# A graph attention kernel: one of four masks per row tile made by ScalarE, another moved from step 4 to step 6

## The chip, the core and the metric

The kernel runs on one core of a Trainium2 chip. The core has five engines that run side by side, each through its own queue of instructions in program order: TensorE (PE in the rows; PEld is its weight load), VectorE (DVE), ScalarE (ACT), GpSimd (POOL) and SyncE (SP), which here only issues DMAs. They meet through semaphores: an instruction adds to one when it is done, and `wait_ge` holds an engine's whole queue until a count is reached. The metric is the time of the kernel on the device in microseconds (us), lower is better.

## The reference

Two graph attention layers over N = 6144 nodes with 128 features, each followed by a sum with its input and a layer norm:

```python
# layer 0
scores = jnp.where(adj > 0, einsum('md,de,ne->mn', x, weight, inp), NEG_PAD)
x = _layernorm(x + jax.nn.softmax(scores / 0.07, axis=1) @ inp)
# layer 1
Wh = x @ W
e = leaky_relu((Wh @ a1)[:, None] + (Wh @ a2)[None, :], 0.2)
att = jax.nn.softmax(jnp.where(adj > 0, e, -9e15), axis=1)
x = _layernorm(x + jax.nn.elu(att @ Wh))
```

`adj` is a 6144 x 6144 matrix of int32 zeros and ones.

## The kernel before

The first part does layer 0, the second, over six groups of 1024 rows, layer 1. The change is in the first part.

**Tiles and steps.** Layer 0 runs over 48 row tiles of 128 rows (`t`), and each tile in 12 steps (`c`) of 512 columns. A tile's work is spread over three passes of the loop, so that in pass `t` the engines work on several tiles: TensorE makes the scores of tile `t` (L563 to L565, three products, since x and z are held as a high and a low float16 part), ScalarE takes the exponential of tile `t-1` (L717), and TensorE transposes the probabilities of a chunk three steps later (L552), ScalarE copies the transposed chunk from PSUM as a high part `pT_hi` (L706), VectorE makes the low part `pT_lo` (L866), and TensorE multiplies both with the values `vals` two steps after the transpose (L528, L530). Blocks 0 to 2 of each tile are turned by DMA instead (`moved_hi`, L711 on ScalarE, `moved_lo`, L417 on GpSimd), so steps 3 to 5 have no transposes on TensorE.

**Masks.** `adj` comes in four quarters of 1536 columns into `adj_sb`. VectorE turns each into `neg_mask` (L830): 0 where there is an edge, -2^60 where there is none. L857, one instruction for two chunks of 512 (a pair, at each odd step), adds mask and scores, writes `rows` and gives a maximum. In pass `t` the masks of quarters 2 and 3 of tile `t` are made at steps 0 and 2, those of quarters 0 and 1 of tile `t+1` at steps 4 and 10. GpSimd makes `edges` from each mask (L394, one byte for each element), which SyncE stores to DRAM for layer 1. `mask_set` counts masks in their order, and SyncE loads the next tile's quarter when the mask of this one is made.

**The end of a tile.** At the last step VectorE takes the row maximum and makes `exp_bias` (L916, L920), for which the exponential of step 0 waits. TensorE's transposes need `pT_lo` of two transposing steps before, since `ps` has two banks for them:

```python
pe.wait_ge(exp_set, C * (t - off) + bc + 1)
after(pe, pT_lo_set, n + 1 - NPT)
```

**The sum of products.** All 12 blocks of a tile are summed in one bank, block 3 first and block 2 last. When they are through, ScalarE copies the bank to `att` at step 8 (`ATT_STEP`, L699). The first block of the next tile is due in the same step 8, and starts the bank afresh:

```python
if bc == MOVED:
    after(pe, att_out, t_of)
```

From `att` VectorE makes the sum with x (L895, L899, step 9), and the statistics (L903 to L908, step 10); GpSimd takes the power -0.5 (L434), and VectorE normalizes at step 0 of the next pass (L911). These run from pass 2 on.

The order of all engines is the order of the code; nothing reorders it.

Of the kernel before, what the change touches and what calls it, by code (L numbers as in the profile page):

```python
# [6 lines left out]
P = 128  # L7
CHUNK = 512
QUARTERS = 4
# [15 lines left out]
EPS = 1e-5  # L25
SPLIT_SCALE = 64.0
MASK_BIG = 2.0 ** 60
PROB_SHIFT = 14 * math.log(2.0)

ALU = mybir.AluOpType  # L30
# [6 lines left out]
def build(nc, x, adj, inp, w0, w1, a1, a2, edge_rows, out):  # L37
# [17 lines left out]
    with ExitStack() as ctx:  # L55
# [19 lines left out]
        s_prod = sb("s_prod", [P, 2, P], F32)  # L75
        a21 = sb("a21", [P, 2], F32)
        consts = sb("consts", [P, GT], F32)
        s_top = sb("s_top", [P, 2], F32)

        def sb0(name, shape, dt):  # L80
# [1 line left out]

        zT = sb0("zT", [P, 2, N], F16)
        adj_sb = sb0("adj_sb", [P, QUARTERS, QW], I32)
        neg_mask = sb0("neg_mask", [P, QUARTERS, QW], BF16)
        neg_mask_row = neg_mask[:].rearrange("p q w -> p (q w)")
        edges = sb0("edges", [P, QUARTERS, QW // 2], U16)
        edge_bytes = edges[:].bitcast(U8)
        vals = sb0("vals", [P, NB, 2 * P], F16)
# [106 lines left out]
        xq_in = sem("xq_in")  # L196
        xr_in = [sem(f"xr_in{i}") for i in range(2)]
        const_set = sem("const_set")
        ident_set = sem("ident_set")
        wT_turned = sem("wT_turned")  # L200
        wT_copied = sem("wT_copied")
# [171 lines left out]
        def _(pool):  # L373
            nc.gpsimd.memset(ident[:], 0.0).then_inc(const_set, 1)
            nc.gpsimd.memset(consts[:], -0.5).then_inc(const_set, 1)
            nc.gpsimd.memset(averager[:], 1.0 / P).then_inc(avg_set, 1)
            nc.gpsimd.memset(w1_c[:, P:P + 1], 1.0 / P).then_inc(avg_set, 1)
            pool.wait_ge(const_set, 2)
# [11 lines left out]
            def make_edges(t, q):  # L390

                after(pool, edges_out[q], 16 * t)
                pool.wait_ge(mask_set, QUARTERS * t + q + 1)
                nc.gpsimd.tensor_scalar(edge_bytes[:, q, :], neg_mask[:, q, :], 1.0 / MASK_BIG, 1.0, ALU.mult,  # L394
                                        ALU.add).then_inc(edges_set, 1)

            for q in range(QUARTERS // 2):
                make_edges(0, q)
# [21 lines left out]
            def tile_rstd(t, par, known):  # L420
                ahead = t < NB - 1
                if t < NB:
                    make_edges(t, 2)
                if t >= 3:
                    score_cols(t - 3)
                if t < NB:
                    make_edges(t, 3)
                if 1 <= t <= NB:
                    moved_low(t - 1)
                if ahead:  # L430
                    make_edges(t + 1, 0)
                if ends_tile(known):
                    pool.wait_ge(ve_set, t - 1)
                    nc.gpsimd.tensor_tensor(small[:, 4:5], small[:, 3:4], consts[:, 0:1], ALU.pow).then_inc(rstd_set, 1)  # L434
                if ahead:
                    make_edges(t + 1, 1)

            tiles(pool, tile_rstd)

# [216 lines left out]

        @block.scalar
        def _(act):
            act.wait_ge(wT_turned, 1)
            nc.scalar.copy(w0T, ps[:, MISC, 0:P])  # L660
            nc.scalar.copy(w1T, ps[:, MISC, P:2 * P]).then_inc(wT_copied, 1)
# [26 lines left out]
            def tile_steps(t, par, known):  # L688
                for c in range(C):
# [10 lines left out]
                    if turn_at(known, c):  # L700
                        off, bc = turn_of(t, c)
                        n = turn_number(t - off, bc)
                        act.wait_ge(turned, n + 1)
                        if n >= PT_SLOTS:
                            act.wait_ge(pv_done, attend_number((n - PT_SLOTS) // TURNS, (n - PT_SLOTS) % TURNS + MOVED) + 1)
                        nc.scalar.copy(pT_hi[:, n % PT_SLOTS, :], ps[:, PT0 + n % NPT, :]).then_inc(pT_hi_set, 1)  # L706
                    if c == MOVED and 1 <= t <= NB:
                        act.wait_ge(exp_set, C * (t - 1) + MOVED)
                        if t >= 2:
                            act.wait_ge(movedT_in[t % 2], movedT_loads(t - 2))  # L710
                        nc.scalar.copy(moved_hi[:], rows[:, (1 - par) * N:(1 - par) * N + MOVED * CHUNK]).then_inc(moved_hi_set, 1)  # L711
# [88 lines left out]
        def _(dve):  # L800
# [23 lines left out]
            def make_mask(t, q, known):  # L824

                dve.wait_ge(adj_in[q], 16 * (t + 1))

                after(dve, masked, PAIRS * (t - 1) + pairs_of(q) if known != 0 else 0)
                after(dve, edges_set, QUARTERS * (t - 1) + q + 1 if known != 0 else 0)
                nc.vector.tensor_scalar(neg_mask[:, q, :], adj_sb[:, q, :], 0.0, -MASK_BIG, ALU.is_le,  # L830
                                        ALU.mult).then_inc(mask_set, 1)

            xT_low(0, 0)
# [4 lines left out]
            def tile_steps(t, par, known):  # L838
                for c in range(C):
# [5 lines left out]
                    if scores_of(known) and c % 2 == 1:  # L845
# [8 lines left out]
                        if k == 0:  # L854
                            after(dve, max_set, t)
                        dve.wait_ge(scored, C * t + c + 1)
                        nc.vector.tensor_tensor_reduce(row_pair(par, k), scores_pair(k),  # L857
                                                       neg_mask_row[:, 2 * k * CHUNK:2 * (k + 1) * CHUNK], 1.0, -3.0e38,
                                                       ALU.add, ALU.max, part_max[:, k:k + 1]).then_inc(masked, 1)
                    if turn_at(known, c):  # L860

                        off, bc = turn_of(t, c)
# [11 lines left out]
                    else:  # L874
                        if c in (0, 2) and scores_of(known):
                            make_mask(t, 2 + c // 2, known)
                        if c in (4, 10) and (known is None or known < NB - 1):
                            make_mask(t + 1, c // 10, None)
                    if c == x_step(known) and (known is None or known < NB - 1):
                        xT_low(t + 1, 1 - par)  # L880
                    if ends_tile(known):
# [180 lines left out]
```

## Time and profile before

| what | value |
|---|---|
| time, median of 3 runs | 1532.46 us (1532.19 to 1532.89) |
| the profiled execution | 1532.11 us, span 1530.3 us |
| TensorE busy | 1442.6 us, 94% of the span, granted clock 0.992 |
| VectorE busy | 1308.3 us, 85% |
| ScalarE busy | 1065.1 us, 70% |
| GpSimd busy | 1009.0 us, 66% |
| chain that ended last | TensorE 70%, VectorE 16%, issue 6%, GpSimd 3% |

The span runs from the first to the last instruction; the time has some 2 us around it. An engine can be busy for most of the span without being the bound, and TensorE's matmuls are pipelined, so its share alone doesn't say how near it is to its limit. The page's 40 slices show two parts: up to slice 26 (about 1000 us) the DMA engines are busy for 0.8 to 0.9 of the time at some 235 GB/s, with the loads of `adj`; after that for 0.2 to 0.5. A busy time of one instruction on ScalarE or VectorE is up to 0.1 us longer than the distance from its start to the next one's, since they overlap a little.

### The profile page before, as it was taken

What the parts mean: (1) busy time and instruction counts of PE and PEld (TensorE: products, weight loads), DVE (VectorE), ACT (ScalarE), POOL (GpSimd) and SP (SyncE); (2) the same over time, 40 slices, a digit from 0 to 9 for tenths busy, and PEclk for the clock granted to TensorE, in tenths of its full rate; (3) what the DMA queues carried; (4) which work ended last, traced back from release to release, by engine and by line L of the source; (5) the groups of instructions that cost most, each with busy time, mean ns of one, the idle gap of its engine ahead of it and who ended that gap; (6) DMA issues with size and microseconds to landing.
All of it is one profiled execution on the core that took longest, in us unless ns stands there. A gap on an engine that the chain in (4) does not pass through costs nothing.

```text
span 1530.3 us, 28253 instructions
## 1 busy us (share of the span) xinstructions
PE 1442.6 (94%) x9853; PEld 1030.4 (67%) x9853; DVE 1308.3 (85%) x2303; ACT 1065.1 (70%) x2327; POOL 1009.0 (66%) x628
## 2 busy tenths in 40 slices
PE   7799999999999999999999999987999999999996
PEld 3477777777777777777777777765566666666664
DVE  6988889988888998888998888976869797979794
ACT  4577887777787777787777787787745454646363
POOL 6545555555555555555555555535999999999995
PEclk9999999999999999999999999998999999999998
DMA  7888888888889988898888898826323534353420
GB/s 243 255 218 249 232 233 243 240 215 242 238 238 222 250 222 236 243 236 231 243 232 225 245 230 234 242 67 128 86 63 70 111 76 108 82 109 80 103 55 14
DMA packets 378749, 278.81 MB, mean 182 GB/s; under 512 B 307696, under 2 KB 354032, under 8 KB 378608
## 3 DMA queue, kind: packets, MB, share of 16 engines
q1 hardware_dynamic: 378608, 277.01, 69.1%
q8 instruction: 79, 1.29, 0.3%
q14 instruction: 62, 0.51, 0.1%
HBM read 160.56 MB, written 40.89 MB: 132 GB/s over the span
## 4 chain that ended last, share of the span: by engine, by line
PE 70%; DVE 16%; issue 6%; POOL 3%; ACT 1%; DVEq 0%; ACTq 0%; POOLq 0%
PE ps L612 11%; PE ps L528 11%; PE ps L605 10%; PE ps L552 9%; PE ps L565 6%; PE ps L564 6%; PE ps L563 6%; DVE pT_lo L866 6%; PE ps L530 5%; PE ps L589 5%; DVE rows L857 4%; DVE neg_mask L830 3%; POOL p_lo L449 2%; DVE xr L895 1%; PE ps L623 1%
## 5 line engine op out<-in xcount | busy, mean ns | idle before, releaser
L717 ACT ACTIVATE rows<-rows,exp_bias 128x512 f32<-128x512 f32 x576 | 415.2, 721 | 81.5 <-DVE exp_bias L920 81.5
L857 DVE CUSTOM_DVE_ANT_0 rows<-ps,neg_mask 128x1024 f32<-128x1024 f32 x288 | 350.7, 1218 | 99.7 <-PE ps L565 99.1
L449 POOL TENSOR_TENSOR p_lo<-p,p_hi 128x1024 fp32r<-128x1024 f32 x180 | 424.3, 2394 | 13.2 <-PE ps L589 7.7
L947 DVE SCALAR_TENSOR_TENSOR p<-ps,e_col,edgesT 128x1024 f32<-128x1024 f32 x288 | 349.0, 1276 | 62.2 <-PE ps L582 37.5
L394 POOL TENSOR_SCALAR edges<-neg_mask 128x1536 uint8<-128x1536 bf16 x192 | 284.4, 1481 | 145.2 <-DVE neg_mask L830 137.3
L706 ACT CAST pT_hi<-ps 128x512 f16<-128x512 f32 x432 | 252.0, 583 | 129.6 <-PE ps L552 121.6
L528 PE MATMUL ps<-vals,pT_hi 128*128 128x256 f16 x1728 | 331.4, 273 | 1.2 <-ACT att L699 0.8
L530 PE MATMUL ps<-vals,pT_lo 128*128 128x128 f16 x1728 | 308.3, 219 | 0.0
L746 ACT CAST p_hi<-p 128x1024 fp32r<-128x1024 f32 x180 | 185.0, 1047 | 176.5 <-DVE p L947 174.4
L552 PE MATMUL ps<-ident,rows 128*128 128x128 f32 x1728 | 263.0, 275 | 39.7 <-DVE pT_lo L866 39.0
L866 DVE TENSOR_TENSOR pT_lo<-ps,pT_hi 128x512 f16<-128x512 f32 x432 | 287.1, 682 | 8.7 <-ACT pT_hi L706 8.7
L434 POOL TENSOR_TENSOR small<-small,consts 128x1 f32<-128x1 f32 x48 | 26.6, 555 | 320.4 <-DVE small L908 320.4
L563 PE MATMUL ps<-zT,xT_hi 128*128 128x512 f16 x576 | 218.9, 380 | 6.9 <-DVE vals L816 4.2
L552 PEld LDWEIGHTS ps<-ident,rows 128*128 128x128 f32 x1728 | 184.4, 141 | 54.0 <-issue 45.8
L564 PE MATMUL ps<-zT,xT_hi 128*128 128x512 f16 x576 | 218.8, 380 | 0.0
L565 PE MATMUL ps<-zT,xT_lo 128*128 128x512 f16 x576 | 218.8, 380 | 0.0
L528 PEld LDWEIGHTS ps<-vals,pT_hi 128*128 128x128 f16 x1728 | 169.1, 98 | 65.9 <-DVE pT_lo L866 1.9
L612 PE MATMUL ps<-p,vals 128*128 128x512 f32 x432 | 204.5, 596 | 0.0
L530 PEld LDWEIGHTS ps<-vals,pT_lo 128*128 128x128 f16 x1728 | 169.1, 98 | 49.4
L830 DVE TENSOR_SCALAR neg_mask<-adj_sb 128x1536 bf16<-128x1536 int32 x192 | 201.3, 1048 | 0.5 <-POOL edges L394 0.3
L417 POOL TENSOR_TENSOR moved_lo<-rows,moved_hi 128x1536 f16<-128x1536 f32 x48 | 176.4, 3675 | 6.5 <-ACT moved_hi L711 2.7
L605 PE MATMUL ps<-p_hi,vals_hi 128*128 128x512 f32 x360 | 157.9, 519 | 6.7 <-POOL vals_lo L445 4.1
(108 smaller groups left out, 1785.6 us busy)
## 6 DMA issues: line engine op xcount, KB each, us to landing
adj_sb<-adj SPq DMA_DIRECT2D x192, 768.0 KB, 4.9
edge_rows<-edges SPq DMA_DIRECT2D x192, 192.0 KB, 4.4
rows<-inp SPq DMA_DIRECT2D x4, 768.0 KB, 9.0
xq<-x SPq DMA_DIRECT2D x48, 64.0 KB, 2.7
xr<-x SPq DMA_DIRECT2D x48, 64.0 KB, 1.9
out<-y_w SPq DMA_DIRECT2D x5, 512.0 KB, 3.7
movedT<-moved_hi SPq DMA_TRANSPOSE x48, 5.5
movedT<-moved_lo SPq DMA_TRANSPOSE x48, 3.8
```

The lines of the kernel that those rows point to most:

```text
L449: nc.gpsimd.tensor_tensor(p1_lo[:, m % LO_SLOTS, :], p1[:, (NB * g + n) % P_SLOTS, :], p1_hi[:, m % HI_SLOTS, :].bitcast(F32), ALU.subtrac ...
L528: nc.tensor.matmul(acc, p_hi, vals[:, jb, :], start=(bc == MOVED and b == 0), stop=False, skip_group_check=True)
L530: mm = nc.tensor.matmul(acc[:, P:2 * P], p_lo, vals[:, jb, 0:P], start=False, stop=(bc == MOVED - 1 and b == BPC - 1), skip_group_check=True)
L552: mm = nc.tensor.transpose(ps[:, PT0 + n % NPT, b * P:(b + 1) * P], rows[:, pb * N + bc * CHUNK + b * P:pb * N + bc * CHUNK + (b + 1) * P] ...
L563: nc.tensor.matmul(scores_bank(c), xT_hi[:, par, :], zT[:, 0, cols], start=True, stop=False)
L564: nc.tensor.matmul(scores_bank(c), xT_hi[:, par, :], zT[:, 1, cols], start=False, stop=False)
L605: mm = nc.tensor.matmul(acc_half(g % 2, i), v[:, k, :], p1_hi[:, m % HI_SLOTS, i * CHUNK:(i + 1) * CHUNK], start=(n == 0 and v is vals1_hi ...
L612: mm = nc.tensor.matmul(acc_half(g % 2, i), vals1[:, n, :], p1[:, (NB * g + n) % P_SLOTS, i * CHUNK:(i + 1) * CHUNK], start=(n == 0), stop ...
L717: nc.scalar.activation(row_chunk(1 - par, c), row_chunk(1 - par, c), ACT.Exp, bias=exp_bias[:, 1 - par:2 - par], scale=EXP_SCALE, accum_ou ...
L857: nc.vector.tensor_tensor_reduce(row_pair(par, k), scores_pair(k), neg_mask_row[:, 2 * k * CHUNK:2 * (k + 1) * CHUNK], 1.0, -3.0e38, ALU.a ...
L866: nc.vector.tensor_tensor(pT_lo[:, s, :], ps[:, PT0 + n % NPT, :], pT_hi[:, s, :], ALU.subtract).then_inc(pT_lo_set, 1)
L947: nc.vector.scalar_tensor_tensor(out=p1[:, (NB * g + n) % P_SLOTS, :], in0=ps[:, R_ROW:R_ROW + 2, :].rearrange("p b w -> p (b w)"), scalar ...
```

## The change

Four things change. The mask is positive: `off_mask` is +2^60 where there is no edge, and L857 (L870 after) subtracts it. GpSimd makes `edges` by one comparison (at most 0) in place of a product and a sum. From pass 1 to pass 46 the mask of quarter 1 of tile `t+1` is made by ScalarE, as Relu(2^60 - 2^60 x adj), at step 7 between `pT_hi` and the exponential, with the constant in a column `big_col`; VectorE no longer makes it at step 10. VectorE's mask of quarter 0 moves from step 4 to step 6. And GpSimd makes `edges` of quarter 1 before the power instead of behind it.

```diff
             def make_edges(t, q):
-                nc.gpsimd.tensor_scalar(edge_bytes[:, q, :], neg_mask[:, q, :], 1.0 / MASK_BIG, 1.0, ALU.mult,
-                                        ALU.add).then_inc(edges_set, 1)
+                nc.gpsimd.tensor_scalar(edge_bytes[:, q, :], off_mask[:, q, :], 0.0, None, ALU.is_le).then_inc(edges_set, 1)
...
                 if ahead:
                     make_edges(t + 1, 0)
+                    make_edges(t + 1, 1)
                 if ends_tile(known):
                     pool.wait_ge(ve_set, t - 1)
                     nc.gpsimd.tensor_tensor(small[:, 4:5], small[:, 3:4], consts[:, 0:1], ALU.pow).then_inc(rstd_set, 1)
-                if ahead:
-                    make_edges(t + 1, 1)
...
                         nc.scalar.copy(pT_hi[:, n % PT_SLOTS, :], ps[:, PT0 + n % NPT, :]).then_inc(pT_hi_set, 1)
+                    if c == 7 and 1 <= t < NB - 1:
+                        q = ACT_QUARTER
+                        act.wait_ge(mask_set, QUARTERS * (t + 1) + q)
+                        act.wait_ge(adj_in[q], 16 * (t + 2))
+                        act.wait_ge(masked, PAIRS * t + pairs_of(q))
+                        act.wait_ge(edges_set, QUARTERS * t + q + 1)
+                        nc.scalar.activation(off_mask[:, q, :], adj_sb[:, q, :], ACT.Relu, scale=-MASK_BIG,
+                                             bias=big_col[:]).then_inc(mask_set, 1)
...
-                nc.vector.tensor_scalar(neg_mask[:, q, :], adj_sb[:, q, :], 0.0, -MASK_BIG, ALU.is_le,
+                if q == ACT_QUARTER + 1:
+                    dve.wait_ge(mask_set, QUARTERS * t + q)
+                nc.vector.tensor_scalar(off_mask[:, q, :], adj_sb[:, q, :], 0.0, MASK_BIG, ALU.is_le,
                                         ALU.mult).then_inc(mask_set, 1)
...
-                                                       neg_mask_row[:, 2 * k * CHUNK:2 * (k + 1) * CHUNK], 1.0, -3.0e38,
-                                                       ALU.add, ALU.max, part_max[:, k:k + 1]).then_inc(masked, 1)
+                                                       off_mask_row[:, 2 * k * CHUNK:2 * (k + 1) * CHUNK], 1.0, -3.0e38,
+                                                       ALU.subtract, ALU.max, part_max[:, k:k + 1]).then_inc(masked, 1)
...
-                        if c in (4, 10) and (known is None or known < NB - 1):
-                            make_mask(t + 1, c // 10, None)
+                        if c in (6, 8) and (known is None or known < NB - 1):
+                            if (c - 6) // 2 != ACT_QUARTER:
+                                make_mask(t + 1, (c - 6) // 2, None)
```

ScalarE's queue in a tile of the middle, before: from `xT_hi` at the end of step 5 to the exponential of step 8.

```order
L674 ACTIVATE xT_hi<-ps 128x128
L706 CAST pT_hi<-ps 128x512
L717 ACTIVATE rows,part_sum<-rows,exp_bias 128x512
L706 CAST pT_hi<-ps 128x512
L717 ACTIVATE rows,part_sum<-rows,exp_bias 128x512
L699 COPY att<-ps 128x256
L706 CAST pT_hi<-ps 128x512
L717 ACTIVATE rows,part_sum<-rows,exp_bias 128x512
```

The same place after, where L709 is `pT_hi`, L728 the exponential and L702 `att`.

```order
L677 ACTIVATE xT_hi<-ps 128x128
L709 CAST pT_hi<-ps 128x512
L728 ACTIVATE rows,part_sum<-rows,exp_bias 128x512
L709 CAST pT_hi<-ps 128x512
L716 ACTIVATE off_mask<-adj_sb,big_col 128x1536
L728 ACTIVATE rows,part_sum<-rows,exp_bias 128x512
L702 COPY att<-ps 128x256
L709 CAST pT_hi<-ps 128x512
L728 ACTIVATE rows,part_sum<-rows,exp_bias 128x512
```

One instruction has come in, ahead of the exponential of step 7 and of `att`.

VectorE's queue before, from `pT_lo` of step 9 to the row maximum at step 11; the ISA rows are L857's pair and its read of the maximum.

```order
L866 TENSOR_TENSOR pT_lo<-ps,pT_hi 128x512
L895 SCALAR_TENSOR_TENSOR xr<-att,small,xr 128x128
L899 SCALAR_TENSOR_TENSOR xr<-att,small,xr 128x128
L866 TENSOR_TENSOR pT_lo<-ps,pT_hi 128x512
L830 TENSOR_SCALAR neg_mask<-adj_sb 128x1536
L903 BN_STATS stats<-xr 128x6
L905 BN_AGGR moments<-stats 128x2
L908 TENSOR_SCALAR small<-moments 128x1
L857 ISA rows,part_max<-ps,neg_mask 128x1024
L857 ISA part_max 128x1
L866 TENSOR_TENSOR pT_lo<-ps,pT_hi 128x512
L916 TENSOR_REDUCE row_max<-part_max 128x1
```

VectorE's queue after, from `xT_lo` of step 5 to the third `pT_lo` (L879) and, in its second half, the same stretch as above.

```order
L832 SCALAR_TENSOR_TENSOR xT_lo<-ps,xT_hi 128x128
L903 TENSOR_SCALAR small<-small 128x1
L879 TENSOR_TENSOR pT_lo<-ps,pT_hi 128x512
L843 TENSOR_SCALAR off_mask<-adj_sb 128x1536
L870 ISA rows,part_max<-ps,off_mask 128x1024
L870 ISA part_max 128x1
L879 TENSOR_TENSOR pT_lo<-ps,pT_hi 128x512 x2
```

```order
L879 TENSOR_TENSOR pT_lo<-ps,pT_hi 128x512
L909 SCALAR_TENSOR_TENSOR xr<-att,small,xr 128x128
L913 SCALAR_TENSOR_TENSOR xr<-att,small,xr 128x128
L879 TENSOR_TENSOR pT_lo<-ps,pT_hi 128x512
L917 BN_STATS stats<-xr 128x6
L919 BN_AGGR moments<-stats 128x2
L922 TENSOR_SCALAR small<-moments 128x1
L870 ISA rows,part_max<-ps,off_mask 128x1024
L870 ISA part_max 128x1
L879 TENSOR_TENSOR pT_lo<-ps,pT_hi 128x512
L930 TENSOR_REDUCE row_max<-part_max 128x1
```

The mask ahead of the statistics is gone, and one stands behind `pT_lo` of step 6, ahead of the pair of step 7.

## Rows read from the trace of the kernel before

The columns of a timeline are the start, the length, the engine, the line, the operation, what it writes and reads, and how often; in brackets the idle time before and what ended it.

**Rows 1.** Busy time by stretch: stretch, length, then each engine's busy us (instructions).

```profile
200.00:1000.00 800.00, 769.41 (x6513) 573.98 (x6512) 710.25 (x1423) 631.22 (x1541) 433.74 (x306) 1.00 0.88 234
```

**Rows 2.** Waits in total: who waited for whom, us, times, longest.

```profile
PE ps L552 <- DVE pT_lo L866: 39.0, 48, 1.4
```

**Rows 3.** Timeline of TensorE, two tiles: start us, length us, instruction.

```profile
499.85 0.61 PE L552 MATMUL ps<-ident,rows 128*128 128x128 f32 x4
...
504.32 0.63 PE L552 MATMUL ps<-ident,rows 128*128 128x128 f32 x4 [0.80 <-DVE pT_lo L866]
...
515.37 0.61 PE L552 MATMUL ps<-ident,rows 128*128 128x128 f32 x4
...
516.47 0.27 PE L528 MATMUL ps<-vals,pT_hi 128*128 128x256 f16 x1
...
517.12 0.61 PE L552 MATMUL ps<-ident,rows 128*128 128x128 f32 x4
```

**Rows 4.** Timeline of VectorE around the edge of a tile, and step 7.

```profile
497.78 1.23 DVE L857 CUSTOM_DVE_ANT_0 rows<-ps,neg_mask 128x1024 f32<-128x1024 f32 x1 [1.07 <-PE ps L565]
...
500.78 0.95 DVE L830 TENSOR_SCALAR neg_mask<-adj_sb 128x1536 bf16<-128x1536 int32 x1
501.64 0.29 DVE L903 BATCH_NORM_STATS2 stats<-xr 128x6 f32<-128x128 f32 x1
...
502.33 1.23 DVE L857 CUSTOM_DVE_ANT_0 rows<-ps,neg_mask 128x1024 f32<-128x1024 f32 x1
...
503.48 0.69 DVE L866 TENSOR_TENSOR pT_lo<-ps,pT_hi 128x512 f16<-128x512 f32 x1
...
515.05 1.23 DVE L857 CUSTOM_DVE_ANT_0 rows<-ps,neg_mask 128x1024 f32<-128x1024 f32 x1 [1.04 <-PE ps L565]
```

**Rows 5.** Timeline of ScalarE, steps 3 to 8 of a tile.

```profile
508.06 1.47 ACT L711 CAST moved_hi<-rows 128x1536 f16<-128x1536 f32 x1
509.44 0.72 ACT L717 ACTIVATE rows<-rows,exp_bias 128x512 f32<-128x512 f32 x1
...
512.51 0.59 ACT L706 CAST pT_hi<-ps 128x512 f16<-128x512 f32 x1
...
514.75 0.73 ACT L717 ACTIVATE rows<-rows,exp_bias 128x512 f32<-128x512 f32 x1
...
515.57 0.37 ACT L699 COPY att<-ps 128x256 f32<-128x256 f32 x1
516.02 0.59 ACT L706 CAST pT_hi<-ps 128x512 f16<-128x512 f32 x1
```

**Rows 6.** ScalarE's groups by form: busy us, mean ns, idle before.

```profile
L746 ACT CAST p_hi<-p 128x1024 fp32r<-128x1024 f32 x180 | 185.0, 1047 | 176.5 <-DVE p L947 174.4
...
L660 ACT ACT_TABLE_LOAD x1 | 1.3, 1283 | 0.7 <-PEq L1051 0.7
```

**Rows 7.** Timeline of GpSimd: first tiles, the tile above, the last mask's tile.

```profile
12.45 4.09 POOL L386 TENSOR_SCALAR vals<-rows 128x1536 f16<-128x1536 f32 x1 [0.69 <-DMA rows<-inp]
...
49.76 1.47 POOL L394 TENSOR_SCALAR edges<-neg_mask 128x1536 uint8<-128x1536 bf16 x1 [0.97 <-DVE neg_mask L830]
...
509.73 1.47 POOL L394 TENSOR_SCALAR edges<-neg_mask 128x1536 uint8<-128x1536 bf16 x1 [0.98 <-DVE neg_mask L830]
511.28 3.70 POOL L417 TENSOR_TENSOR moved_lo<-rows,moved_hi 128x1536 f16<-128x1536 f32 x1
...
1009.80 3.11 POOL L417 TENSOR_TENSOR moved_lo<-rows,moved_hi 128x1536 f16<-128x1536 f32 x1
```

**Rows 8.** Timeline of VectorE: masks that began beside one of these.

```profile
14.94 2.41 DVE L830 TENSOR_SCALAR neg_mask<-adj_sb 128x1536 bf16<-128x1536 int32 x1
...
49.81 2.23 DVE L830 TENSOR_SCALAR neg_mask<-adj_sb 128x1536 bf16<-128x1536 int32 x1
...
510.93 1.08 DVE L830 TENSOR_SCALAR neg_mask<-adj_sb 128x1536 bf16<-128x1536 int32 x1
```

**Rows 9.** DMA issues of the page: KB each, us to landing.

```profile
adj_sb<-adj SPq DMA_DIRECT2D x192, 768.0 KB, 4.9
```

More of the change, by code:

```diff
@@ L27 @@
 MASK_BIG = 2.0 ** 60
+ACT_QUARTER = 1
 PROB_SHIFT = 14 * math.log(2.0)
@@ L77, in build @@
         consts = sb("consts", [P, GT], F32)
+        big_col = sb("big_col", [P, 1], F32)
         s_top = sb("s_top", [P, 2], F32)
@@ L84, in build @@
         adj_sb = sb0("adj_sb", [P, QUARTERS, QW], I32)
-        neg_mask = sb0("neg_mask", [P, QUARTERS, QW], BF16)
-        neg_mask_row = neg_mask[:].rearrange("p q w -> p (q w)")
+        off_mask = sb0("off_mask", [P, QUARTERS, QW], BF16)
+        off_mask_row = off_mask[:].rearrange("p q w -> p (q w)")
         edges = sb0("edges", [P, QUARTERS, QW // 2], U16)
@@ L198, in build @@
         const_set = sem("const_set")
+        big_set = sem("big_set")
         ident_set = sem("ident_set")
@@ L375, in _ @@
             nc.gpsimd.memset(consts[:], -0.5).then_inc(const_set, 1)
+            nc.gpsimd.memset(big_col[:], MASK_BIG).then_inc(big_set, 1)
             nc.gpsimd.memset(averager[:], 1.0 / P).then_inc(avg_set, 1)
@@ L658, in _ @@
         def _(act):
+            act.wait_ge(big_set, 1)
             act.wait_ge(wT_turned, 1)
```

## The prediction

> **What bounds the kernel now.** First the busy time by stretches: from 200 to 1000 us TensorE (PE) is busy 769 of 800 us at a granted clock of 1.00, VectorE (DVE) 710, ScalarE (ACT) 631, GpSimd (POOL) 434 [rows 1]. The second part, some 500 us, is not touched by the change. So the first part is TensorE's, and only what makes TensorE wait, or stops making it wait, counts. Second, the waits by who released them: one dominates, TensorE's transposes L552 waiting for `pT_lo` of L866, 39.0 us in 48 waits, 0.81 us each [rows 2]; 38.5 tiles of such waits are 31 us, all of TensorE's idle time in these 800 us (800 - 769.4). Third, the timeline of one tile, to find that wait and its length in starts. I call step c of the tile loop Sc, by the start of its transposes. S8 and S9 stand at 515.37 and 517.12, so a step with transposes is 1.75 us. S11 is at 499.85; two steps on, S1 of the next tile should start at 503.35 and starts at 504.32: 0.97 us are lost per tile, at its edge [rows 3].
>
> Why there: S1 needs `pT_lo` of step 11, which starts at 503.48 and releases S1 0.84 later. DVE before it has no pause: pair 4 of the masked scores (L857) at 497.78, the step's other work, the mask at 500.78, the statistics at 501.64, pair 5 at 502.33, `pT_lo` [rows 4]. The mask at step 10 is on the path with 501.64 - 500.78 = 0.86.
>
> **What the change removes.** From tile 2 to 46 (45 tiles: tile 1 has no L895 to L908, tile 47 makes no next mask) the mask at step 10 leaves DVE. Pair 4 starts when its scores are there, 1.43 after S9 (517.12 - 515.37 = 1.75, so S9 of this tile is 499.85 - 3.50 = 496.35). Pair 4 to pair 5 took 4.55 and now takes 3.69; 1.15 on to `pT_lo`, 0.84 on to S1: 497.78 + 5.68 = 503.46 against the 503.35 at which TensorE is ready. Pair 5's own scores come at 499.85 + 1.43 = 501.28, before DVE's 501.47, so they don't bind. Of 0.97 us 0.11 stay: 0.86 are won per tile, 38.7 us in 45 tiles. That is the most the change can give, for TensorE has no other idle time.
>
> **What it adds on ScalarE.** The Relu stands between `pT_hi` and Exp of step 7. Behind it in ScalarE's queue stand Exp of step 7 and then the copy `att` of step 8 (L699), and TensorE's products of step 8 (block 3, L520-521) wait for `att_out` of that same copy, since they overwrite the bank that it reads. Now: Exp 514.75, `att` at 515.57 right behind it, ending 515.94; TensorE's products start at 516.47 [rows 3, 5]. The slack is 0.53 us, ScalarE has no idle time between the place of the Relu and `att`, and so all that comes in beyond the slack stops TensorE, in the middle of a step.
>
> Relu's price: no row shows it. From below, the Cast of 128x1536: 1.47, and 1.38 from its start to the next one's [rows 5]. From above, three Exps of 512 columns, 3 x 0.72 = 2.16. I take the Cast's slope from 1024 to 1536 columns ((1.472 - 1.047) / 512 = 0.83 ns a column) on the Exp, which has a bias column too: 0.72 + 1024 x 0.83 ns = 1.57, hence 1.48 start to start [rows 5, 6]. It is nearest to a long Cast, so 1.48 stands far from the upper end.
>
> The Trainium skill (ScalarE: Activation LUTs, What ACT_TABLE_LOAD costs) gives 280 ns + 0.833 ns a column for an ACTIVATE with a bias column, 1560 ns here, and an overlap of 93 ns; by it the term would be 1.47. That page's Rules for kernel authors say to leave relu to VectorE: the mask's 0.95 there against 1.57 here agrees, and by that rule alone the change is a loss.
>
> **When the Relu can start.** At the earliest 514.75, where Exp starts now. But it waits for mask (t+1, 0), since both count `mask_set` up, and that mask moves from step 4 to step 6 on DVE. `pT_hi` of step 6 ends at 512.51 + 0.59 = 513.10, `pT_lo` takes 0.60 to the next start, so the mask is issued at about 513.70. There POOL is inside `moved_lo`. What that does is read from the masks that began beside a POOL instruction: begun 14.94, length 2.41, POOL's op ended 16.54; begun 49.81, length 2.23, POOL's ended 51.23; begun 510.93, length 1.08, POOL's ended 511.20. All three end 0.81 after POOL's instruction does, to 0.01; undisturbed a mask takes 0.95. So a mask waits until POOL's running instruction is through [rows 4, 7, 8]. The reverse shows too: `moved_lo`, issued at 511.28 with the step-4 mask still running, takes 3.70, and 3.11 in the tile with no mask beside it [rows 7]. With step 4 empty, `moved_lo` runs 511.28 to 514.39, and the mask ends at 514.39 + 0.81 = 515.20 instead of 514.65. That is 0.45 later than the Relu could start.
>
> The Trainium skill (GPSIMD Engine Reference, Key points) says that GpSimd shares its SBUF interfaces with VectorE and contends with its 2-port modes. It names no exclusion; if contention only meant a shared rate, the mask would have been slowed by a part and not held to POOL's end. The trace agrees that they contend and goes further.
>
> **Sum.** 515.20 + 1.48 (Relu) + 0.82 (Exp to `att`) + 0.37 (`att`) + 0.15 for two hops between engines = 518.02, against 516.47: TensorE stops for 1.55 us at step 8. The hops have bounds 0 and 0.30 (TensorE started 0.15 after `pT_lo` ended at 504.17). After it all is on time again: `pT_hi` of step 8, 0.45 behind `att`, is masked by TensorE's own delay, pair 4 waits 1.43 from the later S9, and the edge of the tile follows from there with its 0.11. Per tile 1.55 + 0.11 - 0.97 = +0.69; 45 tiles, +31 us. The profiled execution took 1532.1 (span 1530.3), the median of the runs is 1532.5: 1563.
>
> **Costed at nothing.** The mask gone from step 4: pair 2 starts earlier, its scores or `pT_hi` wait. Pair 3 is due at 515.05 [rows 4] and the late mask frees DVE at 515.12. Edges by one comparison: unknown, taken at the 1.47 of the two-op form with the same types and size; from above the 4.09 of the POOL op on 1536 columns [rows 7], from below nothing; POOL idles nearly half of the time and covers all but the top of that. The power (L434) now stands behind `make_edges(t+1, 1)`, which waits for the Relu, done at 516.8, and takes 1.47: POOL is free at 518.3, before S10, while the statistics that it needs stand behind S11, as before. Subtract in L857: L866 subtracts at 0.68 for 512 columns, in line with 1.23 for 1024. SP's order stays; the load of quarter 1 goes out behind the Relu, earlier than behind step 10, and lands in 4.9 us [rows 9], needed a tile later. One ACT_TABLE_LOAD in all, though the second part has Relu and Exp in turns (L764, L767) [rows 6]: no table switch, which would be 2 x 1.28 us per tile.
>
> **Rivals.** (a) The mask is not held by `moved_lo`, whose interior no mask has met: it ends at 513.70 + 0.95 = 514.65, Relu starts at 514.75, and TensorE goes on at 514.75 + 1.48 + 0.82 + 0.37 + 0.10 = 517.52: stop 1.05, per tile +0.19, 1541. For it: only the first part of a `moved_lo` lay beside a mask. Against: the 4.09 us POOL op held one for 1.6 us [rows 7, 8]. (b) No measurable change (within 0.2%, 3 us): all low ends at once, Relu 1.38 from 514.75, no hops: stop 0.85, per tile -0.01, 1532. (c) Faster: TensorE's stop at step 8 does not come, because `att` is not what L528 waits for in fact; then ScalarE's lateness reaches TensorE only by `pT_hi` of step 8 (515.20 + 0.05 + 1.48 + 0.82 + 0.45 = 518.00), `pT_lo` 518.60, pair 4 at 519.20 instead of 518.55: 0.65 + 0.11 = 0.76 lost instead of 0.97, 45 x -0.21, 1523. For it: nearly no wait for `att` is in the trace of before; against: L521 and the 0.53. The two sides part at a stop of 0.86 us. (d) Much slower: Relu at the price of three Exps, +0.59 more per tile, 1590; or slow edges that hold DVE's masks longer.
>
> **How the numbers follow.** Forecast 0.60 (its own range 1554 to 1572, from a Relu 0.1 us shorter or longer and hops of 0 to 0.30), (a) 0.15, (b) 0.07, (c) 0.08, (d) 0.10. The range 1538 to 1575 holds the forecast, (a) and a little of (d), and leaves out (b), (c) and the rest of (d). Faster 0.08, same 0.07, slower 0.85; 0.2% is about what a measurement of this kernel tells from no change.
>
> **What would show it.** TensorE waiting for `att` about 45 times, some 1.4 us each; the wait of L552 for `pT_lo` down to 0.1 or gone; the step-6 mask at 1.5 us instead of 0.95; the Relu at 1.57; a tile longer by 0.69. A step-6 mask at 0.95 speaks for (a); no wait for `att` makes the prediction wrong, as does a tile no longer than before.

## The result, and the profile after

The changed kernel took 1787.4 us (median of 4 runs, 1786.9 to 1788.5) against 1532.6 us before: a ratio of 1.166, 95% interval 1.164 to 1.168. The forecast was 1563 us in a range of 1538 to 1575. The direction was right and the size was off by a factor of eight: +255 us in place of +31.

The same stretch as in [rows 1], from the busy times by stretch of the changed kernel:

```profile
200.00:1000.00 800.00, 652.22 (x5166) 471.26 (x5164) 705.41 (x1103) 543.39 (x1253) 685.07 (x246) 0.96 0.64 187
```

TensorE is down from 769 to 652 us of 800, and GpSimd is up from 434 to 685. No engine is full: VectorE has 705, as it had 710. So the time is in waits. Of the waits in total, the one that answers to [rows 2], and two that are new:

```profile
PE ps L530 <- ACT att L702: 111.5, 46, 2.9
...
PE ps L554 <- DVE pT_lo L879: 106.2, 74, 2.3
...
ACT off_mask L716 <- DVE off_mask L843: 72.0, 46, 2.0
```

The wait for `pT_lo` (now L554 and L879) was to shrink to a tenth and grew from 39 to 106 us; the wait for `att` is there, 46 times, but at 2.4 us each in place of the forecast 1.4. The page's groups name what is new (columns: busy us, mean ns of one, idle before):

```profile
L398 POOL TENSOR_SCALAR edges<-off_mask 128x1536 uint8<-128x1536 bf16 x192 | 783.7, 4087 | 152.9 <-DVE off_mask L843 152.9
...
L843 DVE TENSOR_SCALAR off_mask<-adj_sb 128x1536 bf16<-128x1536 int32 x146 | 273.2, 1872 | 0.1
...
L913 DVE SCALAR_TENSOR_TENSOR xr<-att,small,xr 128x128 f32<-128x128 f32 x48 | 123.1, 2565 | 1.7
```

GpSimd's `edges` take 4.09 us in place of 1.48, 784 us in all. And two VectorE instructions are longer though nothing in them grew: the masks 1.87 us on average (1.05 before), and L913, the second sum of 128 columns at step 9 (L899 before), 2.57 in place of 0.35. In 35 tiles it is L913 that is long, in 10 others the first sum, L909, in its place. VectorE's idle time ahead of the masks is 0.1 us in all, so they don't start late by a semaphore: what grew lies between their start and their end. One tile of TensorE, to be held against [rows 3]:

```profile
540.22 0.61 PE L554 MATMUL ps<-ident,rows 128*128 128x128 f32 x4
...
543.38 0.27 PE L530 MATMUL ps<-vals,pT_hi 128*128 128x256 f16 x1 [1.91 <-ACT att L702]
...
544.04 0.60 PE L554 MATMUL ps<-ident,rows 128*128 128x128 f32 x4
...
547.54 0.61 PE L554 MATMUL ps<-ident,rows 128*128 128x128 f32 x4
...
551.75 0.63 PE L554 MATMUL ps<-ident,rows 128*128 128x128 f32 x4 [2.29 <-DVE pT_lo L879]
...
554.18 0.63 PE L554 MATMUL ps<-ident,rows 128*128 128x128 f32 x4 [0.50 <-DVE pT_lo L879]
...
555.96 0.61 PE L554 MATMUL ps<-ident,rows 128*128 128x128 f32 x4
```

Step 8 starts at 540.22 and step 9 at 544.04: 3.82 in place of 1.75, with the wait for `att` in it. Step 11 to step 0 is 4.21, step 0 to step 1 2.43. That is 2.07, 2.46 and 0.68 us lost at three places. What stands there on VectorE, in the same tile:

```profile
538.59 2.08 DVE L843 TENSOR_SCALAR off_mask<-adj_sb 128x1536 bf16<-128x1536 int32 x1
...
547.60 3.40 DVE L913 SCALAR_TENSOR_TENSOR xr<-att,small,xr 128x128 f32<-128x128 f32 x1
550.92 0.68 DVE L879 TENSOR_TENSOR pT_lo<-ps,pT_hi 128x512 f16<-128x512 f32 x1
```

and on GpSimd:

```profile
535.78 4.08 POOL L398 TENSOR_SCALAR edges<-off_mask 128x1536 uint8<-128x1536 bf16 x1
539.84 3.79 POOL L420 TENSOR_TENSOR moved_lo<-rows,moved_hi 128x1536 f16<-128x1536 f32 x1
543.60 8.13 POOL L398 TENSOR_SCALAR edges<-off_mask 128x1536 uint8<-128x1536 bf16 x2
```

The mask at 538.59 ends at 540.67, which is 0.81 behind the end of the `edges` begun at 535.78 (539.86): the same 0.81 as in [rows 7, 8]. So it is with all 98 masks of this trace that began beside a GpSimd instruction (0.81 or 0.82); the other 48 took 0.95 or 0.96. L913, begun at 547.60, ends at 551.00; two `edges` in a row run from 543.60 to 551.73. And on ScalarE, as in [rows 5]:

```profile
539.11 0.59 ACT L709 CAST pT_hi<-ps 128x512 f16<-128x512 f32 x1 [0.45 <-PE ps L554]
540.70 1.58 ACT L716 ACTIVATE off_mask<-adj_sb,big_col 128x1536 bf16<-128x1536 int32 x1 [1.01 <-DVE off_mask L843]
542.19 0.71 ACT L728 ACTIVATE rows<-rows,exp_bias 128x512 f32<-128x512 f32 x1
...
542.89 0.35 ACT L702 COPY att<-ps 128x256 f32<-128x256 f32 x1
```

The Relu starts behind the mask, at 540.70; `att` follows 2.19 after it.

Other tiles lose more. In the one before, whose stop for `att` was 2.89 us, the granted clock of TensorE falls to the lower of its levels (1.2 GHz) for some 4 us. The columns are the stretch, its length, the busy times of PE, PEld, DVE, ACT and POOL, the granted clock, and the DMA:

```profile
526.00:528.00 2.00, 2.00 (x12) 1.19 (x11) 1.97 (x6) 0.58 (x1) 0.57 (x1) 0.60 0.63 239
528.00:530.00 2.00, 2.00 (x12) 1.49 (x10) 1.97 (x6) 1.15 (x3) 0.09 (x1) 0.54 0.04 8
```

There, step 0 to step 1 is 2.82 (525.75 to 528.57) in place of 2.43, and step 1 to step 2 2.36 (528.57 to 530.93) in place of 1.78. From 200 to 1000 us the mean clock was 1.00 before; with the change it is 0.96.

### The profile page after: what moved, and what is told of

The parts are those of the page before. It is cut to its first block, busy times and chain, and to the rows that moved or that the text cites. A ratio compares the mean times of both kernels' runs of the same rounds, so it can differ in the third digit from the quotient of the medians.

```text
span 1785.0 us, 28349 instructions
## 1 busy us (share of the span) xinstructions
PE 1504.5 (84%) x9853; PEld 1053.6 (59%) x9853; DVE 1529.9 (86%) x2257; ACT 1128.1 (63%) x2373; POOL 1538.7 (86%) x629
## 4 chain that ended last, share of the span: by engine, by line
PE 42%; DVE 32%; issue 14%; ACT 4%; POOL 2%; DVEq 0%; ACTq 0%; POOLq 0%
PE ps L614 10%; PE ps L607 9%; DVE rows L870 8%; DVE off_mask L843 7%; DVE xr L913 7%; DVE pT_lo L879 6%; PE ps L530 5%; PE ps L591 4%; PE ps L554 4%; PE ps L567 2%; PE ps L566 2%; PE ps L565 2%; ACT rows L728 2%; PE ps L532 2%; DVE xr L909 2%
## 5 line engine op out<-in xcount | busy, mean ns | idle before, releaser
L398 POOL TENSOR_SCALAR edges<-off_mask 128x1536 uint8<-128x1536 bf16 x192 | 783.7, 4087 | 152.9 <-DVE off_mask L843 152.9
L728 ACT ACTIVATE rows<-rows,exp_bias 128x512 f32<-128x512 f32 x576 | 414.2, 719 | 70.0 <-DVE exp_bias L934 70.0
L530 PE MATMUL ps<-vals,pT_hi 128*128 128x256 f16 x1728 | 348.6, 282 | 112.4 <-ACT att L702 111.5
L870 DVE CUSTOM_DVE_ANT_0 rows<-ps,off_mask 128x1024 f32<-128x1024 f32 x288 | 350.6, 1218 | 68.6 <-PE ps L567 67.2
L709 ACT CAST pT_hi<-ps 128x512 f16<-128x512 f32 x432 | 251.4, 582 | 236.4 <-PE ps L554 234.2
L554 PE MATMUL ps<-ident,rows 128*128 128x128 f32 x1728 | 277.1, 285 | 107.1 <-DVE pT_lo L879 106.2
L879 DVE TENSOR_TENSOR pT_lo<-ps,pT_hi 128x512 f16<-128x512 f32 x432 | 291.5, 684 | 73.8 <-ACT pT_hi L709 73.7
L532 PE MATMUL ps<-vals,pT_lo 128*128 128x128 f16 x1728 | 323.5, 225 | 0.0
L843 DVE TENSOR_SCALAR off_mask<-adj_sb 128x1536 bf16<-128x1536 int32 x146 | 273.2, 1872 | 0.1
L554 PEld LDWEIGHTS ps<-ident,rows 128*128 128x128 f32 x1728 | 194.0, 147 | 128.7 <-issue 109.2
L565 PE MATMUL ps<-zT,xT_hi 128*128 128x512 f16 x576 | 227.1, 394 | 14.5 <-DVE part_max L870 8.0
L566 PE MATMUL ps<-zT,xT_hi 128*128 128x512 f16 x576 | 227.0, 394 | 0.0
L567 PE MATMUL ps<-zT,xT_lo 128*128 128x512 f16 x576 | 226.8, 394 | 0.0
L913 DVE SCALAR_TENSOR_TENSOR xr<-att,small,xr 128x128 f32<-128x128 f32 x48 | 123.1, 2565 | 1.7
```

What stands on the lines that cost most here:

```text
L398: nc.gpsimd.tensor_scalar(edge_bytes[:, q, :], off_mask[:, q, :], 0.0, None, ALU.is_le).then_inc(edges_set, 1)
L530: nc.tensor.matmul(acc, p_hi, vals[:, jb, :], start=(bc == MOVED and b == 0), stop=False, skip_group_check=True)
L532: mm = nc.tensor.matmul(acc[:, P:2 * P], p_lo, vals[:, jb, 0:P], start=False, stop=(bc == MOVED - 1 and b == BPC - 1), skip_group_check=True)
L554: mm = nc.tensor.transpose(ps[:, PT0 + n % NPT, b * P:(b + 1) * P], rows[:, pb * N + bc * CHUNK + b * P:pb * N + bc * CHUNK + (b + 1) * P] ...
L728: nc.scalar.activation(row_chunk(1 - par, c), row_chunk(1 - par, c), ACT.Exp, bias=exp_bias[:, 1 - par:2 - par], scale=EXP_SCALE, accum_ou ...
L843: nc.vector.tensor_scalar(off_mask[:, q, :], adj_sb[:, q, :], 0.0, MASK_BIG, ALU.is_le, ALU.mult).then_inc(mask_set, 1)
```

## The experiments

**Is it the comparison?** One line of the changed kernel back to a product and a sum (in this section the beginning of such lines is cut and marked with three dots):

```diff
-... off_mask[:, q, :], 0.0, None, ALU.is_le)
+... off_mask[:, q, :], -1.0 / MASK_BIG, 1.0, ALU.mult, ALU.add)
```

> The changed kernel with one line back: edges made from the positive mask by a product with -1/2^60 and a sum with 1, not by the comparison. Theory A (GpSimd's comparison takes 4.09 us instead of 1.48, fills GpSimd and holds VectorE's masks and sums beside it; the rest of the prediction stands): edges 1.48 us, 1563 us, between 1554 and 1572, TensorE waiting for att about 45 times for 1.5 us. Rival B (the loss of 255 us is mostly the Relu in ScalarE's queue and the moved mask): above 1650 us.

1560.9 us (1559.8 to 1561.6), ratio to before 1.018 (1.016 to 1.020). Theory A holds and B falls: 226 of the 255 us are this line. TensorE in that kernel:

```profile
508.90 0.61 PE L555 MATMUL ps<-ident,rows 128*128 128x128 f32 x4
...
511.45 0.27 PE L531 MATMUL ps<-vals,pT_hi 128*128 128x256 f16 x1 [1.30 <-ACT att L703]
...
512.11 0.60 PE L555 MATMUL ps<-ident,rows 128*128 128x128 f32 x4
...
517.36 0.61 PE L555 MATMUL ps<-ident,rows 128*128 128x128 f32 x4
...
519.20 0.63 PE L555 MATMUL ps<-ident,rows 128*128 128x128 f32 x4
```

Step 8 to step 9 is 3.21, a stop of 1.46 for `att` (forecast 1.55), and the edge of the tile, step 0 to step 1, is 1.84, which leaves 0.09 of the old 0.97 (forecast 0.11). The mask at step 6 was held by `moved_lo`:

```profile
507.27 1.47 DVE L844 TENSOR_SCALAR off_mask<-adj_sb 128x1536 bf16<-128x1536 int32 x1
```

Now the other way round, the comparison alone in the kernel before:

```diff
-... neg_mask[:, q, :], 1.0 / MASK_BIG, 1.0, ALU.mult, ALU.add)
+... neg_mask[:, q, :], 0.0, None, ALU.is_ge)
```

> The kernel before, with edges made from its negative mask by one comparison (at least 0) and nothing else changed. Theory A: edges 4.09 us; a tile needs 4 x 4.09 + 3.7 + 0.6 + 1.4 + 0.5 = 22.6 us of GpSimd, more than the 20.77 us of a tile now, so at least 1532 + 47 x 1.8 = 1617 us, with the masks held on VectorE rather 1650 to 1790. Rival B: 1532 to 1545 us.

1886.3 us (1885.9 to 1889.4), ratio 1.231 (1.229 to 1.233). `edges` there:

```profile
L394 POOL TENSOR_SCALAR edges<-neg_mask 128x1536 uint8<-128x1536 bf16 x192 | 784.7, 4087 | 61.9 <-DVE neg_mask L829 61.9
```

The comparison alone costs 353 us, almost 100 over the expected range of 1650 to 1790. GpSimd's busy time from 200 to 1000 us is 635 us, so it isn't full either, and the lower bound of 1617 us from its sum of busy times says little. The masks take 2.71 us on average (1.05 before), and the transposes' wait for `pT_lo` is 199.9 us in place of 39.0. The same line costs 353 us here and 226 in the changed kernel: with slow `edges`, the rest of the change is a gain of 99 us (1886.3 - 1787.4), with fast ones a loss of 28. Why the two differ was not taken apart.

**What makes it slow?** The comparison with a product behind it, and a product alone:

```diff
-... off_mask[:, q, :], 0.0, None, ALU.is_le)
+... off_mask[:, q, :], 0.0, 1.0, ALU.is_le, ALU.mult)
```

> The changed kernel, the comparison kept and followed by a product with 1 in the same instruction. Theory A1 (it is the comparison that is slow on GpSimd): edges at 4 us, 1787 us. Theory A2 (it is the form with one operation that is slow, as the values' product alone takes 4.2 us in the first tile): edges at 1.5 us, 1563 us.

2001.8 us (1997.2 to 2007.7), with `edges` at

```profile
L398 POOL TENSOR_SCALAR edges<-off_mask 128x1536 uint8<-128x1536 bf16 x192 | 1032.5, 5383 | 146.5 <-DVE off_mask L844 146.5
```

Neither theory: the second operation made it slower still.

```diff
-... off_mask[:, q, :], 0.0, None, ALU.is_le)
+... off_mask[:, q, :], 1.0 / MASK_BIG, None, ALU.mult)
```

> The changed kernel with edges made by one product (mask times 1/2^60), no comparison and no second operation; this leaves the inversion out, so edges are 1 where there is none. Theory A1 (comparison): edges at 1.5 us, 1563 us. Theory A2 (one operation): edges at 4 us, 1787 us.

1772.0 us in two runs, with `edges` at

```profile
L398 POOL TENSOR_SCALAR edges<-off_mask 128x1536 uint8<-128x1536 bf16 x192 | 786.0, 4094 | 144.6 <-DVE off_mask L843 134.6
```

So a product alone is as slow as a comparison alone, against theory A1, and by the run before it two operations aren't fast as such, against A2. Eight forms in one kernel (the semaphore waits between them are left out here; the line numbers are added):

```diff
+nc.gpsimd.tensor_scalar(pr_u8[:], pr_bf[:], 0.5, 1.0, ALU.mult, ALU.add)   # L382
+nc.gpsimd.tensor_scalar(pr_u8[:], pr_bf[:], 1.0, 0.5, ALU.add, ALU.mult)   # L384
+nc.gpsimd.tensor_scalar(pr_u8[:], pr_bf[:], 0.5, 1.0, ALU.mult, ALU.mult)  # L386
+nc.gpsimd.tensor_scalar(pr_u8[:], pr_bf[:], 0.5, 1.0, ALU.mult, ALU.max)   # L388
+nc.gpsimd.tensor_scalar(pr_u8[:], pr_bf[:], 1.0, None, ALU.add)            # L390
+nc.gpsimd.tensor_copy(pr_u8[:], pr_bf[:])                                  # L392
+nc.gpsimd.tensor_scalar(pr_h[:], pr_f[:], 0.5, 1.0, ALU.mult, ALU.add)     # L394
+nc.gpsimd.tensor_scalar(pr_h[:], pr_f[:], 0.5, None, ALU.mult)             # L396
```

> The kernel before, with eight GpSimd instructions on scratch tiles of 128x768 ahead of its first one, to read their lengths: from bf16 to bytes product and sum, sum and product, two products, product and maximum, one sum, a copy; from f32 to float16 product and sum, and one product. Theory F (only the pair product and sum is fast): the first and seventh about 0.8 us, the others 2.1 us or more. Rival G (any two arithmetic operations are fast, one alone or a comparison is slow): the first four about 0.8 us. The time itself is 10 to 20 us above the kernel before.

1542.2 us in one run, 9 above the kernel before (1533.0). GpSimd's timeline:

```profile
2.23 0.83 POOL L382 TENSOR_SCALAR pr_u<-pr_bf 128x768 uint8<-128x768 bf16 x1
3.14 0.83 POOL L384 TENSOR_SCALAR pr_u<-pr_bf 128x768 uint8<-128x768 bf16 x1
4.05 0.83 POOL L386 TENSOR_SCALAR pr_u<-pr_bf 128x768 uint8<-128x768 bf16 x1
4.97 2.79 POOL L388 TENSOR_SCALAR pr_u<-pr_bf 128x768 uint8<-128x768 bf16 x1
7.84 2.15 POOL L390 TENSOR_SCALAR pr_u<-pr_bf 128x768 uint8<-128x768 bf16 x1
10.06 0.82 POOL L392 CAST pr_u<-pr_bf 128x768 uint8<-128x768 bf16 x1
10.97 0.83 POOL L394 TENSOR_SCALAR pr_h<-pr_f 128x768 f16<-128x768 f32 x1
11.88 2.13 POOL L396 TENSOR_SCALAR pr_h<-pr_f 128x768 f16<-128x768 f32 x1
```

Product and sum, sum and product, two products, and a copy are fast: 0.82 or 0.83 us for 768 columns. One sum or one product alone is 2.15 and 2.13 us, a product with a maximum 2.79. Product and sum takes the same from bf16 to bytes as from f32 to float16. Theory F is wrong in that sum and product, two products and the copy are fast too, G in that a product and a maximum is not. Each of the eight was run once.

**Where do the slow `edges` hurt?** The comparison for quarters 0 and 1 alone (`if q < 2`), then for quarters 2 and 3 alone (`if q >= 2`), the product and sum for the others:

```diff
+                if q < 2:
                     nc.gpsimd.tensor_scalar(..., 0.0, None, ALU.is_le)
+                else:
+                    nc.gpsimd.tensor_scalar(..., -1.0 / MASK_BIG, 1.0, ALU.mult, ALU.add)
```

> The changed kernel with the slow comparison for the edges of quarters 0 and 1 only, the product and sum for quarters 2 and 3. Theory H (a slow GpSimd instruction costs by what it holds on VectorE): these two stand beside the second sum L914 at step 9, which is then held for about 3 us as in the changed kernel, 45 x 3.0 us more than with fast edges (1561): about 1700 us. Rival P (GpSimd has become the bound by its sum of busy times): half of the slow edges is 5.2 us a tile less of GpSimd, so 1561 us.

1598.4 us (1598.3 to 1599.2): a miss by 100 us, though above the 1561 of rival P. VectorE, and below it GpSimd (in this kernel L913 is the first of the two sums; the second, L917, took 0.35):

```profile
513.73 1.02 DVE L913 SCALAR_TENSOR_TENSOR xr<-att,small,xr 128x128 f32<-128x128 f32 x1
```

```profile
507.34 8.15 POOL L399 TENSOR_SCALAR edges<-off_mask 128x1536 uint8<-128x1536 bf16 x2 [0.98 <-DVE off_mask L847]
```

With quarters 2 and 3 fast, these two `edges` begin 507.34 - 505.71 = 1.6 us behind the start of the step-6 mask, where the changed kernel's begin 5.0 behind (538.59 to 543.60). When a sum of step 9 comes, they have 1.8 us to run (513.73 to 515.49) in place of 4.1 (547.60 to 551.73), and hold it by 0.7 us in place of 3.0. TensorE's wait for `att` is as with fast edges (58.4 us in all against 58.3); the 0.7 us reach it at the edge of the tile:

```profile
515.89 0.63 PE L558 MATMUL ps<-ident,rows 128*128 128x128 f32 x4
...
518.32 0.63 PE L558 MATMUL ps<-ident,rows 128*128 128x128 f32 x4 [0.50 <-DVE pT_lo L883]
```

Step 0 to step 1 is 2.43 in place of the 1.84 with fast edges, and step 11 to step 0 1.84 (514.05 to 515.89) in place of 1.75: 0.68 us a tile, 31 of the 37 us that this kernel is over the 1561.

> The slow comparison for quarters 2 and 3 only. Theory H: these stand beside the masks of steps 2 and 6; the mask of step 2 is held about 1 us longer, that of step 6 is free a little earlier since moved_lo has not begun, and VectorE has slack at step 5: 1565 to 1610 us. Rival P: 1561 us. Should both halves be alike, about 1670 us each.

1679.3 us (1678.0 to 1679.6 in three of four runs, 1704.5 in the other): over the expected range by 70 us. The masks of steps 2 and 6 on VectorE, and TensorE's wait for `att`:

```profile
509.21 2.54 DVE L847 TENSOR_SCALAR off_mask<-adj_sb 128x1536 bf16<-128x1536 int32 x1
...
515.16 2.45 DVE L847 TENSOR_SCALAR off_mask<-adj_sb 128x1536 bf16<-128x1536 int32 x1
```

```profile
520.32 0.37 PE L534 MATMUL ps<-vals,pT_hi 128*128 128x256 f16 x1 [2.89 <-ACT att L706]
```

The step-2 mask is held by the `edges` of quarter 2. What I had counted as a gain, that `moved_lo` has not begun when the step-6 mask comes, is none: the slow `edges` of quarter 3 hold that mask instead, at 2.45 us, longer than `moved_lo` did. The Relu and `att` follow late, and TensorE stops for 2.89 us: 129.7 us of waits for `att` in place of 58.3, at a mean granted clock of 0.95 from 200 to 1000 us. Both sums of step 9 take what they took before (0.34 and 0.35).

The halves cost 37 and 118 us over the 1561 with fast edges, 156 together; both at once cost 226. The other 70 us come only when both are slow. What the traces show of it is that late `edges` of quarters 2 and 3 push those of 0 and 1 onto the sums of step 9, which are then held for 3.0 us in place of 0.7; that this is all of the 70 us is not shown. That rival P is wrong is shown twice.

**The rest of the change, with fast edges.** Four places for the two masks. VectorE's mask back from step 6 to 4:

```diff
-                        if c in (6, 8) and (known is None or known < NB - 1):
-                            if (c - 6) // 2 != ACT_QUARTER:
-                                make_mask(t + 1, (c - 6) // 2, None)
+                        if c == 4 and (known is None or known < NB - 1):
+                            make_mask(t + 1, 0, None)
```

> Edges by product and sum, the Relu at step 7 as in the changed kernel, VectorE's mask of quarter 0 back at step 4. Theory A (at step 6 this mask is held by GpSimd's moved_lo, and the Relu behind it starts 0.4 us late): the Relu waits for nothing, TensorE's wait for att is 0.4 us shorter, 45 x 0.42 = 19 us less than 1561: 1542 us. Rival B (the hold does not reach TensorE): 1561 us.

1537.0 us (1536.3 to 1537.7), 24 us under the 1560.9 with that mask at step 6, and 4 us above the kernel before (ratio 1.002). The waits for `att`, in the kernel with the mask at step 6 and in this one:

```profile
PE ps L531 <- ACT att L703: 58.3, 46, 1.3
```

```profile
PE ps L531 <- ACT att L703: 37.0, 46, 0.8
```

The Relu waits for no mask any more (19.5 us in 45 waits before this edit), and the 21 us that TensorE waits less for `att` are most of the 24. The hold by `moved_lo` is worth 0.53 us a tile, a little more than the 0.42 expected.

The Relu one step later:

```diff
-                    if c == 7 and 1 <= t < NB - 1:
+                    if c == 8 and 1 <= t < NB - 1:
```

> Edges by product and sum, the Relu one step later, behind att and pT_hi of step 8. Theory A: nothing that TensorE waits for stands close behind it: ScalarE is 1.0 us late at step 9 and on time at step 11, 1495 us. Rival B (the Relu's 1.5 us on ScalarE are lost wherever they stand): 1561 us.

1496.0 us (1494.3 to 1496.6), ratio 0.975 (0.974 to 0.977). The same Relu, 65 us less: at step 7 it cost not its own time but what it delayed `att` by. No wait of TensorE for `att` is left in the middle tiles.

No Relu, both masks on VectorE at steps 6 and 8 (the Relu itself and VectorE's wait for it go too, left out here):

```diff
-                            if (c - 6) // 2 != ACT_QUARTER:
-                                make_mask(t + 1, (c - 6) // 2, None)
+                            make_mask(t + 1, (c - 6) // 2, None)
```

> Edges by product and sum, no Relu: both masks of the next tile on VectorE, at steps 6 and 8. Theory A (what is won is the mask's leaving step 10, for VectorE has 1.07 us idle ahead of the pairs of steps 7 and 9): no wait for att, 0.1 us left of the wait of L552, 1495 us. Rival B (VectorE's four masks are too many, wherever they stand): 1525 to 1535 us.

1495.8 us (1494.4 to 1496.5), ratio 0.975 (0.974 to 0.977). The busy times from 200 to 1000 us:

```profile
200.00:1000.00 800.00, 796.40 (x6789) 597.63 (x6788) 751.45 (x1477) 659.84 (x1610) 422.14 (x317) 1.00 0.87 237
```

TensorE is busy 796 of 800 us, and VectorE has more to do than before (751): what counted was where its work stood. The two kernels are alike, so moving a mask to ScalarE brings nothing over moving it to step 8.

The Relu at step 0 of its own tile, ahead of the exponential that waits for `exp_bias`:

```diff
-                    if c == 7 and 1 <= t < NB - 1:
+                    if c == 0 and 2 <= t < NB:
```

(The counts of the four waits are those for tile t, and the edges of quarter 1 stand behind the power again; both are left out here.)

> Edges by product and sum, and the Relu at step 0 of its own tile, ahead of the exponential that waits for the row maximum (GpSimd's edges of quarter 1 behind the power again). Theory A (the Relu costs what it delays the copy att by, and the wait of L552 goes with the mask at step 10): TensorE's wait for att goes, and about 0.86 us a tile are won, 1495 us, up to 1510 if the exponential of step 0 is now late. Rival B (the Relu costs its 1.5 us of ScalarE wherever it stands): 1561 us.

1568.8 us (1566.9 to 1569.2), 74 us over what I expected, and close to rival B's 1561 for another reason. The Relu ends behind VectorE's `pT_lo` of step 0, VectorE's mask of quarter 2 waits for it, GpSimd starts `edges` at the Relu's end, and these hold the next instruction of VectorE. VectorE, then GpSimd:

```profile
521.23 0.96 DVE L845 TENSOR_SCALAR off_mask<-adj_sb 128x1536 bf16<-128x1536 int32 x1 [0.29 <-ACT off_mask L723]
522.11 1.49 DVE L927 TENSOR_SCALAR x_all<-xr,moments,small 128x128 f32<-128x128 f32 x1
```

```profile
521.26 3.81 POOL L398 TENSOR_SCALAR edges<-off_mask 128x1536 uint8<-128x1536 bf16 x2 [2.36 <-ACT off_mask L723]
```

L927, 0.34 us before, takes 1.49. There is a second place: `moved_lo` comes later too, and the step-6 mask beside it takes 2.10 us (begun at 509.13) in place of 1.47. TensorE's waits for both:

```profile
PE ps L532 <- DVE pT_lo L881: 37.4, 46, 0.8
...
PE ps L556 <- DVE pT_lo L881: 23.1, 48, 2.4
```

The first is the stop at step 1, behind L927; the second stands ahead of step 8 (0.44 us at 513.12), behind the step-6 mask. The tile is 21.52 us (499.71 to 521.23 in masks of step 0) against 19.90 with both masks on VectorE. No run takes the two places apart.

**The best version.** Both masks on VectorE, fast edges, and the values' product of the first tile (L386, 4.2 us four times) written as product and a sum of 0:

```diff
-                                        SPLIT_SCALE, None, ALU.mult).then_inc(vals_hi, 1)
+                                        SPLIT_SCALE, 0.0, ALU.mult, ALU.add).then_inc(vals_hi, 1)
```

> Both masks of the next tile on VectorE at steps 6 and 8, edges by product and sum, and the values' high part in the first tile as product and a sum of 0 in place of the product alone. Theory F: four GpSimd instructions of the first 30 us fall from 4.2 to 1.5 us; of these 11 us a part is on the path of the first tile: 1485 to 1493 us. Rival: the loads of the first tile end last, 1496 us as before that edit.

1491.9 us (1491.1 to 1493.0, 5 runs), ratio to before 0.973 (0.972 to 0.975): 2.7% under the kernel before and 16.5% under the changed one. Against the 1495.8 us without the last edit it is 4 us less, but the two intervals of the ratio (0.972 to 0.975, 0.974 to 0.977) overlap. In the traces the first `edges` start at 23.35 us in place of 26.47, which is in line with a gain of that size.

## Why the prediction was wrong

**The step that failed** is a term of the sum that was put at nothing, in "Costed at nothing": "Edges by one comparison: unknown, taken at the 1.47 of the two-op form with the same types and size; from above the 4.09 of the POOL op on 1536 columns". The upper bound was the price, to 0.01 us, and it stood in [rows 7] as a one-operation product on the same number of columns. I chose the row whose types agreed, and the form (how many operations, and which) is what decided. The comparison takes 4.09 us. With that line alone taken back the kernel is at 1560.9: the line is worth 226 us, the whole distance between forecast and result (1787.4 - 1563 = 224).

**Its cover failed too.** "POOL idles nearly half of the time and covers all but the top of that": idle time of GpSimd was no cover, since what a long GpSimd instruction costs is what it holds on VectorE: masks of 1.87 us in place of 1.05, the second sum of step 9 2.57 in place of 0.35, and behind them TensorE's waits of 111.5 us for `att` and 106.2 for `pT_lo`. I had shown that hold in the same text and priced it for one mask and `moved_lo`, but not for the 192 instructions whose length I left open. Rival (d) named it ("slow edges that hold DVE's masks longer") without working out its price; the price that it gave, 1590, was that of a slow Relu alone.

**What was right**, by the kernel with fast edges: 1560.9 for 1563. What the mask at step 10 costs: 0.09 left of 0.97 (0.11 forecast). The Relu 1.577 us (1.57). The step-6 mask held by `moved_lo`: 1.47 (1.50). The stop for `att`: 1.46 (1.55). Per tile 1.46 + 0.09 - 0.97 = 0.58 for 0.69. The subtraction in L870 was free (1218 ns before and after), and there was no second table load. The power at its new place waited for VectorE's statistics, as before. Rival (a), the mask not held, falls by [rows 8] and these. Rival (c), no wait for `att`, falls by 46 waits.

## What to carry to other kernels

Where a trace has two prices for a form of an instruction that it doesn't show, let the form of the operation choose between them. If it can't, take the far end, and follow it through every engine that shares something with this one before you call it covered. In these runs an engine's work cost by what stood behind it in its queue: the same Relu was worth 65 us by one step, and a mask on VectorE cost no more than one on ScalarE once it stood in VectorE's idle time (1495.8 against 1496.0 us). A long GpSimd instruction was a stretch in which some of VectorE's instructions didn't finish.

## What the runs showed of the hardware

- On GpSimd, `tensor_scalar` with product and sum, sum and product or two products, and a copy took 0.82 or 0.83 us for 128x768; product and sum took 1.47 for 128x1536. One product or one sum alone took 2.13 and 2.15 for 768 columns, one product or one comparison 4.09 for 1536. Product and maximum took 2.79 (768), comparison and product 5.38 (1536). A neutral second operation (a sum of 0) made the one product of L386 1.5 to 1.8 us in place of 4.1 to 4.5.
- A VectorE mask begun beside a GpSimd instruction ended 0.81 or 0.82 us after that one's end, in 95 of 95 cases of the kernel before and 98 of 98 of the changed one; begun with none beside it, it took 0.95 or 0.96. The sum of 128 columns with two SBUF inputs was held as well, but ended 0.73 or 0.74 before GpSimd's recorded end (525.00 against 525.73, 551.00 against 551.73, 514.75 against 515.49), and 1.17 before it beside the `edges` of 5.38 us. The normalization L927 (f32, 128 columns) ended 0.08 after it. Why they differ stays open.
- Not held, among others, were two kinds of VectorE instructions that read PSUM: from 150 to 1150 us of the changed kernel 191 pairs L870 and 268 `pT_lo` began beside a GpSimd instruction, and took 1.20 to 1.23 and 0.68 or 0.69 us, as they did alone.
- In the changed kernel TensorE's granted clock fell to the lower level in the tile with stops of 2.89 us (for `att`, at 517.39) and 2.29 us, and not in the next one, with 1.91 and 2.29 us; but it fell again behind stops of 1.98 and 2.29 us (at 595.38 and 603.75). The mean of 200 to 1000 us was 0.96 there, 0.92 with the comparison in the kernel before and 0.87 with comparison and product. In the middle tiles of the kernel with fast edges, where TensorE's longest idle stretch was the 1.3 us for `att`, it was 1.00.
